# First attention of a fused kernel: Q and K rows as two 16-bit parts, and the causal masks added by TensorE

## The reference

```python
def lookup_sin_cos(theta):            # 1024-entry tables over one turn, linear interpolation
    pos = theta / TWO_PI % 1.0 * TABLE_SIZE
    i0f = jnp.floor(pos); frac = pos - i0f
    ...
    s = SIN_T[i0] * (1.0 - frac) + SIN_T[i1] * frac
    c = COS_T[i0] * (1.0 - frac) + COS_T[i1] * frac
    return (s, c)

theta_q = xh / (1.0 + jnp.abs(w_q)) + b_q + t * phi_q     # t is the row's position
Q = jnp.concatenate([cos_q, sin_q], axis=-1)              # 32 numbers a head
theta_k = xh / (1.0 + jnp.abs(w_k)) + b_k + t * phi_k
K = jnp.concatenate([cos_k, sin_k], axis=-1)
theta_v = xh / (1.0 + jnp.abs(w_v)) + b_v
V = cos_v + sin_v
scores = jnp.einsum('bqhd,bkhd->bhqk', Q, K) / scale
scores = jnp.where(causal, -jnp.inf, scores)              # keys behind the query only
attn = jax.nn.softmax(scores, axis=-1)
out = jnp.einsum('bhqk,bkhd->bqhd', attn, V).reshape(B, S, D)
theta_out = out / (1.0 + jnp.abs(w_out)) + b_out
return cos_o + sin_o
```

## Time and profile before

| | us |
|---|---|
| median of 3 runs | 1050.36 (1049.79 to 1055.47) |
| the profiled execution | 1049.52 |
| its span | 1047.6 |
| TensorE busy in the span | 912.2 (87%) |
| VectorE busy | 716.4 (68%) |
| ScalarE busy | 574.1 (55%) |
| GpSimd busy | 299.6 (29%) |
| SP's wait for the first attention to end (L114) | 70.6 |

### The profile page before, as it was taken

How to read it: one execution, slowest core, us unless ns; L and a number is a source line. 1 busy time by engine, 2 the same in 40 slices (tenths; PEclk the granted TensorE clock), 3 DMA queues, 4 the chain that set the end, 5 groups by cost and what they waited for, 6 DMA issues and landing times. The chain is left out here.

```text
span 1047.6 us, 20337 instructions
## 1 busy us (share of the span) xinstructions
PE 912.2 (87%) x7994; PEld 561.8 (54%) x7994; DVE 716.4 (68%) x1404; ACT 574.1 (55%) x1030; POOL 299.6 (29%) x293
## 2 busy tenths in 40 slices
PE   1587989799579789999789999998799988999997
PEld 0232333333147545565456777776689974455554
DVE  7986774615678989887768889886678764344412
ACT  3478688878478553552145555554678753332410
POOL 1222333212137231000237667666153210000000
PEclk9997889899779999999989999999899999999999
DMA  5406050320131030000130000000200000000001
GB/s 153 72 1 81 1 74 8 45 38 1 50 113 41 2 131 1 2 2 1 34 131 2 3 2 2 2 2 2 71 2 2 2 2 1 1 6 16 21 1 41
DMA packets 20573, 30.34 MB, mean 29 GB/s; under 512 B 5936, under 2 KB 15870, under 8 KB 19328
## 3 DMA queue, kind: packets, MB, share of 16 engines
q1 hardware_dynamic: 18368, 26.96, 11.2%
q10 hardware_dynamic: 2112, 2.10, 0.6%
HBM read 18.56 MB, written 2.10 MB: 20 GB/s over the span
## 5 line engine op out<-in xcount | busy, mean ns | idle before, releaser
L542 ACT ACTIVATE t_pT<-t_sc 128x1536 f32<-128x1536 f32 x96 | 137.5, 1454 | 48.9 <-PE t_sc L635 48.1
L635 PE MATMUL t_sc<-t_qk 32*128 32x512 f32 (+3 forms) x768 | 123.6, 603 | 43.7 <-DMA t_qk<-t_sines 26.0
L3149 PE MATMUL f_psh<-f_h,fs_w 128*128 128x512 f16 x512 | 114.4, 379 | 1.5 <-DVE f_h L3093 1.5
L3093 DVE SCALAR_TENSOR_TENSOR f_h<-f_psh,f_h 128x512 f16<-128x512 f32 x64 | 43.8, 690 | 100.8 <-ACT f_h L3119 100.7
L635 PEld LDWEIGHTS t_sc<-t_qk 32*128 32x128 f32 x768 | 56.6, 209 | 102.3 <-ACT t_pT L542 47.0
L261 POOL TENSOR_SCALAR_AFFINE_SELECT t_pT<-t_pT 128x512 f32<-128x512 f32 x64 | 61.2, 977 | 170.5 <-ACT t_pT L542 170.3
L3119 ACT ACTIVATE f_h<-f_psh 128x512 f16<-128x512 f32 x64 | 38.2, 597 | 108.4 <-PE f_psh L3149 108.4
L2612 POOL TENSOR_SCALAR_AFFINE_SELECT r_att<-r_att 128x1024 f16<-128x1024 f16 x64 | 69.5, 1108 | 68.5 <-DVE r_att L2652 68.3
L655 PE MATMUL t_ot<-t_pT,t_v 128*17 128x512 f32 (+3 forms) x768 | 74.6, 505 | 10.1 <-DVE t_ou L394 8.5
L3149 PEld LDWEIGHTS f_psh<-f_h,fs_w 128*128 128x128 f16 x512 | 49.8, 98 | 59.0 <-issue 2.0
L1908 PE MATMUL c_pso<-ck_VO,c_pT 128*128 128x256 f16 x480 | 55.0, 273 | 1.4 <-DVE c_pT L1759 1.4
(11 more groups left out here) (510 smaller groups left out, 2056.2 us busy)
## 6 DMA issues: line engine op xcount, KB each, us to landing
t_qk<-t_cosines SPq DMA_DIRECT2D x24, 128.0 KB, 5.6
t_qk<-t_sines SPq DMA_DIRECT2D x24, 128.0 KB, 7.0
x<-in_x ACTq DMA_DIRECT2D x4, 512.0 KB, 6.8
out_x<-x SPq DMA_DIRECT2D x4, 512.0 KB, 2.9
r_rcos<-in_ret_cos SPq DMA_DIRECT2D x1, 1280.0 KB, 8.0
r_rsin<-in_ret_sin SPq DMA_DIRECT2D x1, 1280.0 KB, 10.6
t_qk<-t_cosines SPq DMA_DIRECT2D x16, 64.0 KB, 2.3
t_qk<-t_sines SPq DMA_DIRECT2D x16, 64.0 KB, 2.3
```

Of the source, the lines that this page charges most:

```text
L542: a.activation(pT[:, at:at + 3, :].rearrange("p a s -> p (a s)"), sc[s % 2][:], ACT.Exp, scale=CURVE * CURVE / math.sqrt(2 * DH)).then_inc ...
L635: last = t.matmul(sc[s % 2][:, 512 * k + at:512 * k + at + w], qk[r, g % 3, 1, P * i:P * i + P], qk[r, g % 3, 0, q0:q0 + w], start=(part = ...
L3093: v.scalar_tensor_tensor(dst[:, 1], psh[:, i % BANKS, :], 0.0, dst[:, 0], ALU.max, ALU.subtract).then_inc(lo_done, 1)
L3149: last = mm(psh[:, i % BANKS, :], l, r, start=(k == 0), stop=(k == len(todo) - 1))
```

## The change

- The Q and K rows are now `parts`: the f32 value rounded to f16, and the rest, again f16. For group 0 ScalarE rounds (`a.copy`), for the others VectorE (`tensor_copy`, a cast); VectorE subtracts. The new tiles `cos_parts` and `sin_parts` are moved into `qk`, in as many bytes as before.
- A score step multiplies three times in 16 bits: high by high, high by low, low by high.
- A bf16 identity times a bf16 matrix `future`, -1e14 above the diagonal, is added to each diagonal block in PSUM. GpSimd's masks and their semaphore go, and `weigh` waits for the exponential alone.
- Group 1's transposes and its angles come earlier, at (0, 3), since `sines` and `cosines` are free as soon as the parts are made. `sums` moves ahead of the two halves, `row_gains` behind them, and on VectorE `prepare(1)` ahead of `post_v(0)`.
- For quad 0 ScalarE issues the moves of the sines.

```diff
+        ident_low, future = sb("ident_low", [P, P], BF16), sb("future", [P, P], BF16)
-        qk = sb("qk", [P, 3, 2, S])
+        qk = sb("qk", [P, 3, 2, 2, S], F16)
+        cos_parts, sin_parts = sb("cos_parts", [P, 2, 2, S], F16), sb("sin_parts", [P, 2, 2, S], F16)
-        TURN_AT = {(0, 8): 1, (2, 2): 2, (4, 2): 3}
+        TURN_AT = {(0, 3): 1, (2, 2): 2, (4, 2): 3}
...
+        def moves(g, c, lo, hi):
+            for hh in range(4):
+                at, to = 64 * (g % 2) + 16 * hh, 32 * hh + 16 * c
+                yield qk[to:to + 16, g % 3, :, :, lo:hi], (cos_parts, sin_parts)[c][at:at + 16, :, :, lo:hi]
...
             for h in range(2):
                 for g in range(2):
                     for c in range(2):
-                        if g == 0:
-                            sp.wait_ge(bent, 2 * pieces_of(0, h) - 1 + c)
+                        if g == 0 and c == 1:
+                            continue
+                        sp.wait_ge(bent, 2 * pieces_of(0, h) - 1 + c)
...
+            own.link(g.memset(future[:], 0.0))
+            g.affine_select(out=future[:], in_=future[:], compare_op=ALU.is_ge, fill=FUTURE, base=0,
+                            pattern=[[1, P]], channel_multiplier=-1).then_inc(future_ready, 1)
             inverse_root(1)
-            for q in range(QUADS):
-                for s in (0, 1, 2, 7, 8):
-                    mask(SLOTS * q + s)
...
             def post_qk(n, h=None):
...
+                    v.scalar_tensor_tensor(piece(w, h), f, CURVE_OFF, piece(w, h), ALU.add, ALU.mult).then_inc(formed, 1)
+                if n:
+                    v.wait_ge(formed, 2 * pieces_of(n, h))
+                    for w, _, parts in sides:
+                        v.tensor_copy(parts[:, :, 0, lo:hi], cut(w, lo, hi)).then_inc(rounded, 1)
+                for c, (w, _, parts) in enumerate(sides):
+                    v.wait_ge(rounded, 2 * pieces_of(n, h) - 1 + c)
+                    v.tensor_tensor(parts[:, :, 1, lo:hi], cut(w, lo, hi), parts[:, :, 0, lo:hi], ALU.subtract).then_inc(bent, 1)
...
             def turn_step(n, h=None):
...
                 if n:
-                    for g in (2 * n - 2, 2 * n - 1):
-                        a.wait_ge(moved[g % 3], moves_of(g))
-                if n == 1:
-                    a.wait_ge(first, 16 * 8)
+                    a.wait_ge(bent, 2 * pieces_of(n - 1))
...
+            for h in range(2):
+                waves_qk(0, h)
+                for c, (w, parts) in enumerate(((cosines, cos_parts), (sines, sin_parts))):
+                    a.wait_ge(formed, 2 * pieces_of(0, h) - 1 + c)
+                    a.copy(parts[:, :, 0, 512 * h:512 * h + 512], ...).then_inc(rounded, 1)
+                if h == 0:
+                    move_sines(0)
...
                     exp_step(EXPS * g + e)
+                    if (g, e) == (0, 1):
+                        move_sines(1)
...
-                for part in range(2):
+                for part, (of_k, of_q) in itertools.product(range(2), ((0, 0), (0, 1), (1, 0))):
                     for slot, h, k in chunks:
...
+                for slot, h, k in chunks:
+                    for j, i, at, w in PIECES[slot % SLOTS]:
+                        if P * i == 512 * j + 512 - w:
+                            last = t.matmul(sc[s % 2][:, 512 * k + at:512 * k + at + P], ident_low[:], future[:],
+                                            start=False, stop=True, skip_group_check=True)
                 last.then_inc(filled, 1)
...
-                if s in DIAGONAL:
-                    t.wait_ge(masked, masks_before(slot) + 1)
-                else:
-                    t.wait_ge(stepped, AT[("exp", exps_for(slot), None)] + 1)
+                t.wait_ge(stepped, AT[("exp", exps_for(slot), None)] + 1)
```

More of the change, by code:

```diff
@@ L1 @@
 from contextlib import ExitStack
+import itertools
 import math
@@ L29 @@
 MASKED = -1e15
+FUTURE = -1e14
 P_BIAS = 7 * math.log(2.0)
@@ L191, in moves_of @@
             return 16 * 8 * (g // 3 + 1 + (g % 3 == 1))
-        def masks_before(slot):
-            return 5 * (slot // SLOTS) + sum(s in DIAGONAL for s in range(slot % SLOTS))
         def part_of(w, n):
@@ L217, in move @@
             def move(g, c, lo, hi, done):
[L219 to L222, removed]
+                for dst, src in moves(g, c, lo, hi):
+                    sp.dma_start(dst, src).then_inc(done, 16)
             for h in range(2):
@@ L349, in post_qk, with cut, parts_free @@
                 f = piece(frac, h)
+                lo, hi = (0, S) if h is None else (512 * h, 512 * h + 512)
                 v.wait_ge(sin_pre, pieces_of(n, h))
-                for w, waves in ((cosines, cos_waves), (sines, sin_waves)):
+                if n:
+                    parts_free(n)
+                sides = ((cosines, cos_waves, cos_parts), (sines, sin_waves, sin_parts))
+                for w, waves, _ in sides:
                     v.wait_ge(waves, pieces_of(n, h))
-                    v.scalar_tensor_tensor(piece(w, h), f, CURVE_OFF, piece(w, h), ALU.add, ALU.mult).then_inc(bent, 1)
+                    v.scalar_tensor_tensor(piece(w, h), f, CURVE_OFF, piece(w, h), ALU.add, ALU.mult).then_inc(formed, 1)
+                if n:
+                    v.wait_ge(formed, 2 * pieces_of(n, h))
[4 more added lines that the diff above has]
+                    v.tensor_tensor(parts[:, :, 1, lo:hi], cut(w, lo, hi), parts[:, :, 0, lo:hi], ALU.subtract).then_inc(bent, 1)
+            def cut(w, lo, hi):
+                return w[:].rearrange("p (k s) -> p k s", k=2)[:, :, lo:hi]
+            def parts_free(n):
+                for g in (2 * n - 2, 2 * n - 1):
+                    v.wait_ge(moved[g % 3], moves_of(g))
+                if n == 1:
+                    v.wait_ge(first, 16 * 8)
             def pre_v(n):
@@ L438, in _ @@
             v.tensor_copy(rec[:, 0, 0:1], recs[:, 0, 0:1]).then_inc(recs_ready, 1)
+            sums(1, 0, 3, 4)
+            sums(1, 1, 4, TB)
             for h in range(2):
@@ L449, in _ @@
                     post_qk(0, 0)
-            sums(1, 0, 3, 4)
-            sums(1, 1, 4, TB)
+            post_qk(0, 1)
+            variances(1)
             v.wait_ge(s_row, 16 * 4)
             row_gains(0, 0, 1, slice(0, 128))
-            post_qk(0, 1)
-            variances(1)
             pre_v(0)
-            row_gains(0, 0, 1, slice(128, D))
-            row_gains(1, 2, 3, slice(0, D))
-            v.wait_ge(rs_ready, 2)
-            v.wait_ge(mean_ready, 2)
-            normalise(TB, 2 * TB, xn_next)
-            post_v(0)
-            pre_v(1)
             def prepare(n):
@@ L476, in _ @@
             prepare_rest(1)
+            post_v(0)
+            row_gains(0, 0, 1, slice(128, D))
+            pre_v(1)
+            row_gains(1, 2, 3, slice(0, D))
+            v.wait_ge(rs_ready, 2)
+            v.wait_ge(mean_ready, 2)
+            normalise(TB, 2 * TB, xn_next)
             for g in range(1, QUADS):
@@ L566, in copy_o, with move_sines @@
                 a.copy(oT[:, j, :], ot[j][:]).then_inc(ot_copied, 1)
+            def move_sines(h):
+                a.wait_ge(bent, 2 * pieces_of(0, h))
+                for dst, src in moves(0, 1, 512 * h, 512 * h + 512):
+                    a.dma_start(dst, src).then_inc(moved[0] if h else first, 16)
             a.wait_ge(nm_ready, 1)
```

26 lines of the change are left out of this document (12 added, 14 removed).

## The result

The changed kernel takes 1059.82 us (median of 6 runs, 1056.98 to 1061.88); before took 1050.07 in the same comparison. The ratio is 1.009, 95% interval 1.0058 to 1.0123: **slower by 0.9%**, where 1067 (+17) was predicted. The profiled execution has a span of 1058.1 us, 10.5 more than before's, and a mean granted clock of 0.943.

A forecast was written before the change was run, and what follows sets the result against it. TensorE was taken as the bound in most of a quad, with VectorE nearly without slack in quads 1 and 3. Terms +1 + 6.0 + 5.4 + 3.4 + 2.5 - 1.2 = +17.1 gave 1067 us, range 1051 to 1079.

The forecast's parts named there:

- start of quad 0: Quad 0: later sine moves and post_v(0) behind group 1's angles delay group 1's cosines by 6.0 us (bounds +3.4 to +8.7).
- stalls, quads 1 and 3: VectorE's casts and subtractions make front_o late, so TensorE waits at slot 2: +5.4 us in quad 1, +3.4 in quad 3.
- half clock behind them: After the stalls in quads 1 and 3 TensorE's clock can fall: 1.5 + 1.0 us taken, bounds 0 and 7.
- TensorE's steps, quads 2 and 4: Scores and masks on TensorE taken as +1 us; first weighings of quads 2 and 4 wait less for VectorE, -1.2.
- exposed loads: Score steps in two pieces (slots 1, 2 and 8): weight loads outlast the columns they serve, 5.4 us in all.
- The masks' price: TensorE's masked score steps: 56 ns for each of 256 matmuls, 0.1 us per step for the change of tiling.
- My condition for being wrong: Wrong if first weighing starts before 62 us, stalls in quads 1 and 3 are absent, or warm masked steps are under 1.07.
- The fourth rival: Masks cost TensorE nothing, falling where it waits for ScalarE; the whole 25.6 us of passes counts: 1040 us, chance 0.10.
- rival 1: The clock stays up after the new stalls and in quad 0's six weighings: -2.6 - 2.5, so 1062 us; chance 0.15.
- rival 2: 32-row weight loads no faster in 16 bits and tiling changes cost double: scores and masks +12, 1078 us; chance 0.10.
- rival 3: Quad 0's start and the VectorE stalls hardly show, casts taking 0.70 us: 1047 to 1052 us, chance 0.15.

The follow-up runs named there:

- both edits: Changed kernel with front_o(g-1, 1) directly behind post_qk in quads 1, 3 and 5, and group 0's waves_v(0) and post_v(0) earlier: 1041.19 us, ratio to before 0.9927.

## Why the prediction was right, and where its terms were not

The direction held, and the place of the loss too. Against the span's +10.5 the terms were:

| term | predicted | measured | how |
|---|---|---|---|
| start of quad 0 | +6.0 | +2.2 | C1 |
| stalls, quads 1 and 3 | +5.4, +3.4 | +5.2, +3.2 | slot 2's end behind C1 and C2: 18.7 to 24.0, 20.7 to 23.9 |
| half clock behind them | +2.5 | +6.7 | rest of C1-T2 and C2-T3 |
| TensorE's steps, quads 2 and 4 | -0.2 | -6.8 | the other intervals (-5.8) and what follows (-1.0) |

- **Stalls: right.** The casts read 1.23 us; `front_o` came 22.9 us behind the cosines (23.1 said), and moving `front_o` took 15.8 us away, more than the whole loss.
- **The clock: right in kind, under-sized by 4.2.** I had put its full price at 3.5 us each time and then taken 1.5 + 1.0, within bounds of 0 and 7. It fell both times, and stayed at 0.50 for some 8 and 9 us of work. Filling the wait gave back 3.5 and 3.9: the full price was right, the discount wrong. The 6.7 of the table is a remainder, which TensorE's quicker steps in these intervals lower.
- **The start: the term that failed**, +2.2 where even its lower bound was +3.4. The first weighing came at 64.17, not 66.7, and the cosines 17.5 us behind it, not 18.8. My step had ScalarE issue the moves at 41.2, behind its exponentials; they went out from 38.67 on, and the third step came at 43.79, not 45.6. The rest is VectorE, 12.7 us for the angles instead of 13.1, and the six weighings in 7.2 us, not 7.9.
- **TensorE's steps: mis-sized.** I computed 0.853 us of streaming and 0.21 for latency and tiling. The step fell by 0.32, not 0.213, to 0.75, and two-piece steps cost no more: the 5.4 us of exposed loads don't exist. The masks' price (0.055 each, 0.11 a step) was right. So a masked step of six came at 1.20, where 1.3 stood. My condition for being wrong, masked warm steps under 1.07, was met by steps with two masks (0.97) and by those with three where the transposes follow at once (0.93), not by those with four to six (1.09 to 1.20). The -6.8 holds something more, which no term had: before's own spell at half clock in quad 2 (0.50 in 120:124) is gone from T2-C2, some 2.0 us (29.72 for 27.76 with `front_o` moved, which has no such spell), and 1.0 stands behind the stage. That leaves 3.8 for the steps.
- **The fourth rival** (masks free) is half true, and for another reason. The masks fall in part where TensorE waits, but for VectorE. Of the others, rival 1 (the clock stays up) fell with the 0.50 behind both stalls, rival 2 (slow 16-bit loads) with the step of 0.75, and rival 3 (the stalls hardly show) with the waits of 6.68 and 5.74 us.

The terms' errors, -3.8, -0.4, +4.2 and -6.6, leave 17.1 at 10.5. The start's and the clock's cancel, which is luck: the total is nearer than its parts. The direction didn't hang on it, as one moved line, which removed the two stalls, took back more than the whole loss. Not settled is how the C1-T2 interval divides exactly between waiting and clock, since a quicker TensorE only meets the next wait.

## What to carry to other kernels

When one engine is made faster at the cost of more work on another, look for the places where the other one had half a microsecond of slack. Here 7 us of new work on VectorE stood ahead of a result that TensorE needed: the stalls grew by 8.4 us, and the clock behind them took some 7 more. One line moved in VectorE's list turned a loss of 0.9% into a gain of 0.7%. A filling that is placed by hand fits one timing only; when the wait moves, it can stand in the way.

## What the runs showed of the hardware

- Stalls of 6.68 and 5.74 us were followed by a granted clock of 0.50 for some 8 and 9 us of unbroken matmuls; the same stalls filled with matmuls by zeros left it at 1.00. Shorter waits were followed by a fall as well: 2.84 us (0.51 in 100:104, both edits) and 2.55 us (0.50 from 120 to 128, the masks on GpSimd).
- ScalarE's queue issued DMAs (0.6 us each for the first three) while its activations ran.
- The f16 loads of 32 rows kept the weight load busy for 32 ns each (37.1 us / 1152; one takes 99 ns, they overlap), hidden even where a load serves 128 columns (steps of 0.76 us in two pieces, 0.75 in one).
- With the masks on GpSimd some of VectorE's instructions took 1.59 us where they took 1.23 without.
- The same code behind the stage took 771.0 to 777.8 us in the 14 profiled executions.
